# Reordered first blocks, an x load in three parts, half of the first norms on GpSimd, and paired steps from step 4 in a float32 attention and feed-forward kernel

## The reference

```
x = x + _layernorm(_L0_attn_ref(_layernorm(x), w_q, w_k, w_v, w_o))
x = x + _layernorm(_L0_ffn_ref(_layernorm(x), W_r, W_k, W_v, mu_r, mu_k))
# attention: q, k, v = x @ w.T; 16 heads of 16; softmax(q k^T / 4) v; @ w_o.T
# ffn: xr, xk mix each token with the one before by mu
#      sigmoid(xr @ W_r.T) * (square(relu(xk @ W_k.T)) @ W_v.T)
```

## Time and profile before

| | us |
|---|---|
| median of 3 runs | 1211.97 (1211.91 to 1216.13) |
| the profiled execution, device time | 1211.89 |
| its span in the trace | 1209.9 |
| PE busy in the span | 1185.9 |
| ACT busy | 1055.9 |
| DVE busy | 787.4 |
| POOL busy | 271.9 |

### The profile page before, as it was taken

One profiled execution on the slowest core, in us unless ns is written; L12 is line 12 of the kernel. 1 busy time (PEld: TensorE's weight loads), 2 busy tenths in 40 slices (PEclk: granted clock), 3 DMA queues, 4 the chain that ended last, 5 costly groups with the idle time before them and its releaser, 6 DMA issues.

```text
span 1209.9 us, 25798 instructions
## 1 busy us (share of the span) xinstructions
PE 1185.9 (98%) x10604; PEld 648.8 (54%) x10604; DVE 787.4 (65%) x1838; ACT 1055.9 (87%) x1405; POOL 271.9 (22%) x351
## 2 busy tenths in 40 slices
PE   7999999999999999999999999999999999999997
PEld 4544555555555555455554555555554555545454
DVE  7553757758575765847567575767668465554757
ACT  4789998999989999998998989899898989989872
POOL 2000213222221322222222222223222222222121
PEclk9999999999999999999999999999999999999999
DMA  4447564317622294215734165321972149401000
GB/s 161 117 127 191 111 135 87 107 54 140 113 64 89 62 179 93 76 49 121 143 72 122 50 129 119 74 89 54 161 119 57 33 109 154 89 1 32 6 19 18
DMA packets 61799, 112.72 MB, mean 93 GB/s; under 512 B 6512, under 2 KB 31344, under 8 KB 61616
## 3 DMA queue, kind: packets, MB, share of 16 engines
q1 hardware_dynamic: 61360, 109.60, 40.3%
q10 hardware_dynamic: 288, 1.05, 0.3%
HBM read 68.42 MB, written 41.94 MB: 91 GB/s over the span
## 4 chain that ended last, share of the span: by engine, by line
PE 93%; DVE 3%; ACT 2%; DMA 1%; issue 0%; POOL 0%; SPq 0%; DVEq 0%
PE O L526 39%; PE M L508 28%; PE M L465 23%; PE M L407 3%; PE M L435 2%; ACT PT L616 2%; DMA xA<-x_dram 1%; DVE sth L818 1%; DVE xB L965 0%; DVE A L826 0%; DVE QS L781 0%; ACT QS L644 0%; POOL rsh L1187 0%; DVE mvh L821 0%; DVE st L767 0%
## 5 line engine op out<-in xcount | busy, mean ns | idle before, releaser
L616 ACT ACTIVATE PT<-M 128x1024 f32<-128x1024 f32 x1274 | 1000.9, 866 | 109.7 <-PE M L508 99.4
L508 PE MATMUL M<-QS,KS 50*128 50x512 f32 x2048 | 497.4, 419 | 7.9 <-ACT PT L616 7.9
L526 PE MATMUL O<-PT,V 128*17 128x512 f32 x4096 | 490.6, 595 | 0.4 <-ACT PT L616 0.4
L508 PEld LDWEIGHTS M<-QS,KS 50*128 50x128 f32 x2048 | 220.2, 184 | 263.4 <-ACT PT L616 237.0
L526 PEld LDWEIGHTS O<-PT,V 128*17 128x17 f32 x4096 | 93.2, 96 | 229.4 <-issue 209.3
L465 PE MATMUL M<-xnT,WH 64*128 64x512 f32 x496 | 142.7, 405 | 0.0
L1185 POOL TENSOR_SCALAR veh<-mvh 128x2 f32<-128x2 f32 x96 | 21.4, 223 | 422.6 <-DVE mvh L821 420.8
L1087 DVE SCALAR_TENSOR_TENSOR A<-Z,M 128x512 f32<-128x512 f32 x30 | 20.6, 687 | 109.8 <-PE M L465 109.8
L465 PE MATMUL M<-WH,xnT 64*128 64x256 f32 x480 | 84.0, 283 | 0.0
L465 PE MATMUL M<-WH,C 64*128 64x256 f32 x480 | 83.7, 284 | 0.0
L465 PE MATMUL M<-WH,cT 64*128 64x256 f32 x480 | 83.5, 284 | 0.0
(11 more groups left out here) (155 smaller groups left out, 1701.9 us busy)
## 6 DMA issues: line engine op xcount, KB each, us to landing
scr<-p SPq DMA_DIRECT2D x124, 256.0 KB
QS<-scr SPq DMA_DIRECT2D x56, 256.0 KB, 5.8
KS<-scr SPq DMA_DIRECT2D x56, 256.0 KB, 10.2
QS<-scr SPq DMA_DIRECT2D x70, 128.0 KB, 6.1
KS<-scr SPq DMA_DIRECT2D x68, 128.0 KB, 8.0
xA<-x_dram SPq DMA_DIRECT2D x16, 512.0 KB, 7.2
xB<-x_dram SPq DMA_DIRECT2D x16, 512.0 KB, 7.8
out_dram<-xB SPq DMA_DIRECT2D x15, 512.0 KB, 3.7
```

Source lines behind the costliest of these rows:

```text
L508: e.matmul(PM[bank[i, j]], KS[qd][rows, pair, kt * 128:kt * 128 + 128], QS[qd][rows, pair, hf * 512:hf * 512 + 512], start=True, stop=True) \
L526: ins = e.matmul(PO[32 * j:32 * j + 17, :], V[b % 2][:, kt, 4 * qd + j, :], PT[i % 3][:, j, :], start=(kt == 0), stop=(kt == 7))
L616: e.activation(PT[i % 3][:, j:k + 1, :], PB[:, at:at + len(numbers), :], ACT.Exp, scale=SCALE) \
```

## The change

It changes the first unit's order and what leads to it. The tables and the norms, cut to their core:

```diff
-PAIRED = 12
+PAIRED = 4
-FIRST = {2: "V2", 3: "K01", 4: "V3", 5: "Q10", 6: "K10", 7: "K11", 8: "Q01", 9: "Q11", 12: "T0", 18: "T1", 20: "Q00",
-         22: "K00", 24: "Q01", 26: "K01"}
+FIRST = {4: "K10", 6: "Q10", 8: "K11", 12: "T0", 14: "Q01", 16: "Q11", 20: "T1", 22: "Q00", 24: "K00", 26: "Q01",
+         28: "K01"}
-ALONE = ("T00", "T01", "D00", "E00", "T10", "D10", "T11", "E10", "V0", "E01", "E11")
-ALONE_IN = {0: ("V1", "Q00"), 1: ("K00",)}
+ALONE = ("T00", "T01", "D00", "E00", "D10", "E10", "V0", "V1", "T10", "T11", "Q00", "E01", "E11")
+ALONE_IN = {0: ("K00",), 1: ("V2",), 2: ("V3",), 3: ("K01",)}
+IN_SCORES = {"V0": 2, "V1": 3}
-SENT = ("Q00", "K00", "K01", "Q10", "K10", "K11", "Q01", "Q11")
+SENT = ("Q00", "K00", "K01", "K10", "Q10", "K11", "Q01", "Q11")
-FIRST_SPREADS = {2: [(1, (0, 1), (0,))], 6: [(1, (1,), (1,))], 7: [(2, (0, 1), (0,))], 8: [(2, (1,), (1,))],
-                 10: [(3, (0, 1), (0,)), (3, (1,), (1,))], 16: [(qd, (0,), (1,)) for qd in range(4)]}
+FIRST_SPREADS = {0: [(1, (0,), (0,))], 1: [(1, (1,), (0,))], 4: [(1, (1,), (1,))], 8: [(2, (1,), (0,))],
+                 10: [(2, (0,), (0,))], 11: [(3, (0, 1), (0,))], 12: [(2, (1,), (1,)), (3, (1,), (1,))],
+                 20: [(qd, (0,), (1,)) for qd in range(4)]}
...
-            warm(3)
+            warm(6)
+            alone(("T00", 0))
+            alone(("T01", 0))
...
+            e.dma_start(xA[:, 2:4, :], x[0, 256:512, :].rearrange("(t p) c -> p t c", p=128)) \
+                .then_inc(*up(xa0_in, ("xA0", 0), by=16))
             e.dma_start(wide, wpack[:, 3588:4612]).then_inc(*up(wide_in, ("wide_in",), by=16))
...
             ln1_stats(0, 0)
-            ln1_stats(0, 1)
+            ln1_tiles(0, 1)
             ln1_norm(0, 0)
...
-            ln1_norm(0, 1, (0, 1))
             after_T(("T00", 0), 0, True)
             after_T(("T01", 0), 0, True)
+            ln1_means(0, 1)
...
             ln1_rsqrt(0, 0)
+            lower_part("wv")
             ln1_rsqrt(0, 1)
+            for t in range(4, 8):
+                p.wait_ge(("ln1_r", 0, 1))
+                e.tensor_scalar(xA[:, t, :], xA[:, t, :], mv[:, t, 0:1], rs1[:, t:t + 1], ALU.subtract, ALU.mult) \
+                    .then_inc(*up(pool_wrote, ("xn_tile", 0, t), *([("xn", 0, 1)] if t == 7 else [])))
+            lower_part("wq")
+            lower_part("wk")
```

More of the change, by code:

```diff
@@ L96, in plan @@
             continue
-        batch = 0 if i < 11 else owner(word, u)
-        at = [i] if i < 9 else [i, i + 1]
-        then = [i + 1] if i < 8 else [i + 2] if i == 9 else [j for j in range(at[-1] + 1, i + 12) if j < STEPS and not turns[j]][:2]
+        batch = 0 if i < 20 and word[0] in "QK" else owner(word, u)
+        at = [i] if i < PAIRED else [i, i + 1]
+        then = [i + 1] if i < PAIRED else [j for j in range(at[-1] + 1, i + 12) if j < STEPS and not turns[j]][:2]
         for row, steps in ((0, at), (1, then)):
@@ L145, in banks @@
     for word in ALONE:
-        take((word, 0), free)
-        free.append(left((word, 0)))
+        if word in IN_SCORES:
+            of[word, 0], freed[word, 0] = IN_SCORES[word], None
+        else:
+            take((word, 0), free)
+            free.append(left((word, 0)))
     for i in range(PAIRED):
@@ L159, in banks @@
             of[i, j], freed[i, j] = j, ("exp", i - 1, j) if i else None
+    for word, k in IN_SCORES.items():
+        freed[0, k] = left((word, 0))[1]
     fifth, free = free[0], free[1:]
@@ L179, in banks @@
         if not TURNS[i]:
-            free += [left(piece) for piece, _ in ENDS[i + 1]]
+            free += [left(piece) for piece, _ in ENDS[i] + ENDS[i + 1]]
     of[TAIL[0], UNITS - 1], freed[TAIL[0], UNITS - 1] = number[4], at[4]
@@ L579, in tensor @@
                 .then_inc(*up(pe_wrote, ("how_many",)))
-            for word in ("T11", "E10", "V0", "E01", "E11"):
+            for word in ("V1", "T10", "T11", "Q00", "E01", "E11"):
                 alone((word, 0))
@@ L639, in first @@
                     pr, n = at
[L640 to L645, removed]
+                    dst, cols = (QS, KS)["DE".index(word[0])][0], slice(512 * n, 512 * n + 512)
+                    for a in range(2):
+                        rows = slice(64 * a, 64 * a + SHIFT)
+                        e.activation(dst[rows, pr, cols], m[rows, :], ACT.Copy) \
+                            .then_inc(*up(act_wrote, ("hi", piece, a)))
                 elif word[0] == "V":
@@ L687, in scalar @@
             first("T01")
-            parted("wv")
-            for word in ("D00", "E00", "T10", "D10", "T11", "E10"):
+            for w in ("wv", "wq", "wk"):
+                parted(w)
+            for word in ALONE[2:]:
                 first(word)
-            parted("wq")
-            parted("wk")
-            first("V0")
             exponentials(0, 0, 1)
@@ L836, in after_T @@
                     if not head:
[L837 removed]
+                        p.wait_ge(("piece", piece), ("piece", ((("Q10", "Q11"), ("V1", "V3"))[b > 1][g], b - 1)))
                         e.tensor_copy(xnT[0][:, c, cols], m[:, :]).then_inc(*note(("hi", piece)))
@@ L844, in after_T @@
                 else:
-                    p.wait_ge(("bank", piece), ("piece", ((("K10", "Q11"), ("V1", "V3"))[b > 1][g], b - 1)))
+                    p.wait_ge(("bank", piece), ("piece", ((("Q10", "Q11"), ("V1", "V3"))[b > 1][g], b - 1)))
                     e.tensor_copy(xnT[0][:, c, cols], On[:, :]).then_inc(*note(("hi", piece)))
@@ L864, in after_DE @@
                 cols, dst, m = slice(n * 512, n * 512 + 512), (QS, KS)[i][0], PM[bank[piece]]
-                if n:
-                    for a in range(2):
-                        rows = slice(64 * a, 64 * a + SHIFT)
-                        p.wait_ge(("piece", piece))
-                        e.tensor_copy(dst[rows, pr, cols], m[rows, :]).then_inc(*note(("hi", piece, a)))
                 for a in range(2):
@@ L1258, in load_xa @@
             def load_xa(b):
-                for g in range(2):
+                for g in range(0 if b else 1, 2):
                     if b:
@@ L1327, in sync @@
             top(0, 0, 0)
+            store(("Q00", 0))
             for i in range(STEPS):
```

78 lines of the change are left out of this document (40 added, 38 removed).

## The result

| | before | with the change |
|---|---|---|
| median, us | 1211.94 (4 runs) | 1221.80 (4 runs, 1221.60 to 1224.62) |
| ratio | | 1.0073, 95% interval 1.0054 to 1.0092 |
| the profiled execution, us | 1211.89 | 1224.62 |
| its span | 1209.9 | 1222.7 |

The kernel before was run once more beside the change, hence its four runs. (The two medians alone would give 1.0081, inside the interval.) By the medians the change makes the kernel about 9.9 us slower. That is beyond the 0.5% that this kernel's measurement can tell, and outside the range.

The account below looks back on a forecast made before the run. PE, busy 98% of the span, was taken as the bound, so gains must come from its own sequence. The terms -0.65 - 5.2 + 3.5 + 3.3 = +0.95 on 1211.9 gave 1212.9 us; 8 in 10 range 1206.5 to 1216.6.

Parts of the forecast that it names:

- the 5.9 us gained: Up to steps 12 and 13: 0.65 gained by step 3 and 5.2 in steps 4 to 13.
- `values` of steps 18 and 19: PE's timeline after both waits for transfers: expected at 84, where it was 83.43 before.
- The prologue: Start of the kernel up to the first scores: x and norms earlier, `values` of step 3 at 42.35, 0.65 gained.
- 7.2 for the second block: Load of x in the prologue: its second block lands at 7.2 us, before at 8.77.
- POOL's norms: Second-half norms moved to POOL: at most 1.31 each, done two us before T10's turn; a rival (0.02) had 1218.
- The pairs: Steps 4 to 13 run as pairs of 4.4 us: 21.8 us for what took 27.03, 5.2 gained.
- once as before: T1's pair, now at step 20, comes once as before; a pair with T was put at 4.61 us.
- The first wait: PE at step 16 wants Q's spread at 66.85, but it lands at 70.3: 3.5 us lost.
- The second wait: PE at step 20 wants quad 2's second K half at 79.15; it lands at 82.5: 3.3 lost (1.7 to 5.1).
- Four issues (1.7) and a landing in that traffic end at 82.5: SP's spread of quad 2's second K half, issued from 76.7: landing between 80.9 and 84.3, middle taken.
- an error in the prologue shifts everything by itself: Both losses hang on K10's end plus 32 us of transfers, while a pair-pace error in steps 8 to 18 shifts nothing.
- The third rival: Chance 0.16: landing at 84.3 adds 1.8, slow clock behind the second wait adds 1.7, giving 1216.4.

Follow-up runs that it names:

- experiment 4: The changed kernel with the 512 KB load of `A` moved from ACT's queue to SP's, behind x and the constants: 1222.36 us, ratio 1.0084.
- experiment 6: experiment 5 with the load of `A` moved to SP's queue as in experiment 4: 1207.12 us, ratio 0.9958.
- experiment 7: experiment 6 with the copy of E11 given back from ACT to DVE, as before the change: 1205.56 us, ratio 0.9947.
- experiment 9: experiment 7 with quad 1's outputs in the first unit turned at step 17 again, not 19: 1206.03 us, ratio 0.9947.
- experiment 12: experiment 9 with seven warming matmuls in place of six: 1205.00 us, ratio 0.9946.
- experiment 10: experiment 5 with `PAIRED` back at 12 from 4, so paired steps start at step 12: 1216.56 us, ratio 1.0034.
- experiment 2: The changed kernel with quad 2's second K half spread ahead of quad 3's spreads and xB: 1218.26 us, ratio 1.0050.
- experiment 5: The changed kernel with quad 2's first K half spread behind Q10's store and its second ahead of quad 3: 1209.53 us, ratio 0.9978.
- experiment 8: experiment 3 with 24 filling matmuls at each wait instead of 15: 1223.47 us, ratio 1.0094.
- experiment 3: The changed kernel with 15 filling matmuls on PE ahead of the waiting scores of steps 17 and 21: 1223.22 us, ratio 1.0082.
- experiment 1: The changed kernel with stores in batch 0 no longer waiting for the landing of earlier spreads: 1216.78 us, ratio 1.0039.
- experiment 11: experiment 5 with eight warming matmuls ahead of the first pass in place of six: 1211.62 us, ratio 0.9991.

## Why the prediction was wrong

It was right in kind: two waits of PE, one for QS and one for KS, in SP's order as written, that take back the 5.9 us gained. It was wrong in size: 1212.9 forecast, 1221.8 measured, 8.9 more. At `values` of steps 18 and 19 the forecast had 84.0 and the trace has 92.53, which is 8.5 of it.

| term | forecast | measured | off, us |
|---|---|---|---|
| `values` of step 3 | 42.35 | 44.08 | +1.7 |
| step 3 to steps 12, 13 | 21.8 | 22.28 | +0.5 |
| store K10 home | 56.9 | 58.95 | +2.05; K10 2.6 late, its store 5.36 for 5.8 |
| K's spread landed | 60.7 | 62.72 | link 3.8, measured 3.77 |
| store Q10 home | 66.5 | 68.70 | link 5.8, measured 5.98 |
| Q's spread landed | 70.3 | 73.42 | link 3.8, measured 4.72: +0.9 |
| second K half issued | 76.7 | 80.07 | +3.4, nearly all inherited |
| second K half landed | 82.5 | 89.25 | link 5.8, measured 9.18: +3.4 |
| landing to `values` 18, 19 | 1.7 | 3.28 | +1.6, the clock |

**The prologue** missed by 1.7: step 3 came 1.1 us later than before (44.08 for 43.00), where 0.65 was to be gained. The step that failed is "7.2 for the second block": it landed at 8.83. The first block did come early, at 4.46 for 4.6. With the load of `A` moved away from ACT's queue it landed at 7.56, 8.08, 7.36, 7.37 and 7.59 (experiments 4, 6, 7, 9, 12), in the other eight kernels with this x load at 8.8 to 9.7, one profile each. So what delayed it was that load in flight beside it. This agrees with the Trainium skill's sentence that the issuing engines share the same 16 DMA engines (DMA: Bandwidth & Descriptors, Issuing engines are not separate DMA queues), which the prediction had weighed only for the first block. What followed from it: D00 at 14.23 for 12.95. The second pair of scores stood at 31.29 for 30.0. The other 0.4 lies in steps 1 and 2, which have a V piece: they took 3.44 and 3.46 for the 3.25 forecast.

**POOL's norms** cost nothing, as said: 1.21 each, the last ended at 21.30, and T10 started at 23.27.

**The pairs** were right: 22.28 us for 21.8 (the first pair took 4.51 for 4.0), against 27.03 before; experiment 10 shows 4.0 of these 4.75 with nothing but `PAIRED` changed. T1's pair was not "once as before": 5.81 for 4.61, the 1.2 by which the `values` at its start ran slow (3.12 for 1.91). Where the clock held it took 5.17 (experiment 2), with the wait of 0.5 for `On` that experiment 9 removes; the change's own trace has no such wait.

**The first wait** was forecast as 3.5 and was 4.24. K10's second half was done at about 52.8 for 50.25, and its store's way was 5.36 for 5.8. The later links held within 0.2, but for Q's spread, 4.72 for 3.8; why that one took longer is open (3.9 in experiment 5). Experiment 5 shows the chain as cause: with the stores ahead of the spreads it needs no landing between them, and the waits are gone.

**The second wait** is the step that failed most, the term "Four issues (1.7) and a landing in that traffic end at 82.5". From the first issue to the landing it took 9.2 us where 5.8 were forecast, outside the bounds of 4.2 to 7.6. From 73.44 to 89.25 the DMA engines moved 166 GB/s on average, so 2.6 MB. The forecast's upper bound, 84.3, had 2.2 MB at the 181 GB/s of the earlier trace rows: K11's store (0.5), eight spreads of quad 3 (0.8), xB (0.5) and the half itself (0.4). The four spreads of quad 3 that SP issues behind it are the 0.4 MB more. At 181 GB/s that is 2.2 us, and the store started 1.2 later, which makes 87.7; the last 1.5 is about what the lower rate gives. This is an estimate from bytes: no run takes only those four spreads away. I had also taken the middle of two bounds where the upper one, the crowded one, was the state of things. In experiment 2, where it goes first, no one waits for it. The landing also inherited 3.1 us of lateness from the first chain, as the prediction had said it would ("an error in the prologue shifts everything by itself").

**The clock.** The third rival had the mechanism, with a chance of 0.16: 1.7 us behind the second wait, and nothing behind the first, "the second would absorb this". The first was 1.6 at `values` of steps 18 and 19, 3.28 us after the landing for 1.7, and another 1.2 in T1's pair behind them. The second held: experiment 8 kept the first 3.2 us and gained nothing by it. The Trainium skill's rule (TensorE: Matmul & The Clock Gate, HAM oscillation), that a wait for a transfer lets the next block start cold, agrees with the 0.50 granted behind the 4.24 us wait. Not every wait for a transfer does it: behind 1.41 us in experiment 10 the clock stayed at 1.00. I had left it to a rival although the one row on it spoke for it and none against. It belonged in the forecast.

What decided was that three errors of the same sign add up along one chain, up to `values` of steps 18 and 19: prologue, pairs and K10's store 2.1, the later links 4.7 (3.4 of it the second landing), clock 1.6. The range took the bounds of each by itself, so it ended at 1216.6.

## What to carry to other kernels

Where one queue issues stores and loads that wait for each other, write its waits down as a chain and look at the order before the work around it is pulled forward. A store behind a load that it doesn't need costs the load's whole way, here 3.8 us in the chain; with the second K half's place in the queue and the slow clock behind the waits it was 12.3 us, and two entries of a table gave that back. When a wait of some microseconds is forecast on the engine that sets the time, count the slow clock behind it, and add the late terms of one chain instead of bounding each alone. Before a small edit is called worthless, look how far its gain got: the load behind x brought x 1.3 us earlier, and in the profiled run a fallen clock took that back before step 3; in another version the same edit went with 2.4 us.

## What was not expected of the hardware

- The slow stretch outlasts the wait. Behind 4.24 us of idling the clock stood at 0.50 from 72 to about 81.4 us with PE busy all the time from 73.4 on; behind 3.15 us it came back at about 95.
- Short waits can start one as well, and not every time. The clock fell behind waits for a transfer of 1.5 to 2.1 us in experiments 3 and 8 and of 1.45 in experiment 1, and stayed at 1.00 behind 1.41 in experiment 10, at the same place. Of the ten kernels with a wait of 1.7 us for the first exponentials it fell in the profiled runs of three (experiments 4, 6 and 11); it fell behind no wait of 0.9. This may be one cause of runs of the same kernel that lie several microseconds apart. Each kernel has one profile here, so that isn't shown, and experiment 11 shows that holding the clock in the first wait alone doesn't narrow them.
- Matmuls over 50 rows into a bank that is overwritten later kept the clock at 1.00 for the five microseconds in which the scores had nothing to work on (experiment 8).
- The four spreads of a K half of quad 2, 0.4 MB, took 3.8 us from the first issue to the landing for the first half, by themselves, and 9.2 us for the second, between other spreads, at a DMA share of 1.0 to 1.1.
